# Relative-position scores with eight queries in three 128-row stationaries instead of two queries in one of 96 rows

## The chip, the cores and the metric

The kernel runs on one core of a Trainium2 chip. Times are device microseconds (us) of one execution. Five engines work side by side: TensorE (PE, with its weight loads as PEld), VectorE (DVE), ScalarE (ACT), GpSimd (POOL) and SyncE (SP), which here issues every DMA.

## The reference

An attention layer with relative positions, then a routed feed-forward layer, on 16 sequences of 1024 rows and 256 columns, 16 heads of 16. The part that the change is about are the attention scores:

```
idx = r[None, :] - r[:, None] + (MAX_LEN - 1)          # jax clips it to the table's 1023 rows
rel = rel_emb[idx]
qk = jnp.einsum('bhld,bhrd->bhlr', q, k) / np.sqrt(HEAD_DIM)
qk = qk + jnp.einsum('bhld,lrd->bhlr', q, rel)
att = jax.nn.softmax(qk, axis=-1)
out = jnp.einsum('bhlr,bhrd->bhld', att, v)
```

The first einsum is the content term, the second the rel term. For a query l the rel term needs, for each key r, the table's row r - l: a window of the table that moves by one with the query.

## The kernel before, in words

A tile is 128 queries of one sequence with all 16 heads; there are 128 tiles (8 per sequence). Within a tile 16 groups g = 0 to 15 follow each other: jp = g // 4 picks 256 of the 1024 keys, i = k = g % 4 picks 32 of the 128 queries. A group's scores fill two PSUM banks, c = 0 and 1, each 128 keys by 16 heads by 32 queries, and `scores(g, c, buf)` fills one of them. Below, one such call is called a pass; a tile has 32.

A product of float32 numbers is made of three fp16 products (high and low halves), so 16 dimensions take 48 rows of contraction, and 96 rows hold two such blocks. **Content term:** a pass has 8 matmuls, one for two heads: the stationary is `ks` (96 rows by 128 keys, the two heads above each other), the moving operand is `qm`, 64 columns, which is zero where block and head don't match. **Rel term:** a pass has 16 matmuls, one for two neighbouring queries. The stationary is 128 columns of `tw`, in which the second block of rows is the table shifted by one; the moving operand is `rm`, 16 heads by two queries, 32 columns, zero where block and query don't match. `tw_s` is the shifted table in DRAM, `raw` the six loads (SP, `load_raw`) of a tile's queries, repeated down the 96 rows. `mask(i)` on POOL makes `qm` and `rm` of 32 queries out of `raw` with two multiplications by 0/1 masks.

One group on PE, as `tile` writes it: pass c = 0 of g; a transpose of the last group's row maxima (`transpose_max`, L674, which waits on DVE's L962); pass c = 1 of g; work of other stages (`wide` and `mixed`: products with the values L693, transposes L700 and L705, projections L714); then `shift` (L683), which adds the negated maxima of the last group to its banks. In four groups of a tile with k = 1, and in g = 0 and 8, `wide` comes straight after pass c = 1. In the ten others PE first waits on `s_nmr`, which DVE's L971 raises; L971 itself needs `transpose_max`. DVE does for a group: L971 (negated maxima), L974, the reduction L962 of the group's two banks, then `side(g)`, small operations of the other stages (layer norms, router). ACT does the exponential (L847). POOL's order within a tile is written out in its `tile`: mask(3), splits of x1 and x, `wp` to `osum` (L580 to L590), `qkb` to `qkl` (L594, L547, L549), and so on, then x1 (L625), mask(0), rs2 (L541, L543), mask(1), mask(2). SP's order is written out too: the window of keys 3, `load_raw` once mask(3) is done, `xr`, windows 0 to 2, the stores.

Before the attention loop come the constants, the writes of `tw_s`, eight tiles of projections alone, and the first loads. The attention loop of every engine but SP has three tiles in its body (`passes`, NBUF = 3) and is jumped back 42 times.

Of the kernel before, what the change touches and what calls it, by code (L numbers as in the profile page):

```python
# [24 lines left out]
TWC = 3 * P  # L25
NU = 2 * L
# [3 lines left out]
NBUF = 3  # L30

# [7 lines left out]
def sandwich_kernel(nc, x, wqT, bq, wkT, bk, wvT, bv, woT, bo, relT, baseT, base_b,  # L39
# [9 lines left out]
    t_s = nc.dram_tensor("t_s", (2, HD, NU + 1), f16, kind="Internal").ap()  # L49
    tw_s = nc.dram_tensor("tw_s", (ROWS, NU), f16, kind="Internal").ap()  # L50

    ctx = ExitStack()
    with ctx:
# [11 lines left out]
        mask_q = sb("mask_q", [ROWS, H, IW], f16)  # L65
        mask_r = sb("mask_r", [ROWS, H, IW], f16)
# [132 lines left out]
        s_raw = sem("s_raw")  # L199
        s_mask = sem("s_mask")  # L200
# [82 lines left out]

        assert (NT - 2) % NBUF == 0

        def passes(eng, tile):
            tile(-TPB, 0, att=False, proj=True, a=False, b=False)
            with eng.Fori(1, TPB) as n:
                tile(n - TPB, n, att=False, proj=True, a=False, b=False)
            tile(0, TPB, att=True, proj=True, a=False, b=False, ph=0)  # L290
            tile(1, TPB + 1, att=True, proj=True, a=True, b=False, ph=1)
            with nc.Fori(2, NT, NBUF, engines=(eng.engine,), hint_back_edge=True) as t:
                for k in range(NBUF):
                    tile(t + k, t + (k + TPB), att=True, proj=True, a=True, b=True, ph=(2 + k) % NBUF)
            tile(NT, None, att=False, proj=False, a=True, b=True, ph=NT % NBUF)
            tile(NT + 1, None, att=False, proj=False, a=False, b=True)
# [3 lines left out]
        def _(sp):  # L300
# [31 lines left out]
            for s in range(2):  # L332
                for k, part in enumerate(SPLIT_ST):
                    r = (3 * s + k) * HD
                    sp.dma_start(tw_s[r:r + HD, :], t_s[part, :, 1 - s:1 - s + NU]).then_inc(s_tws, 16)
            sp.wait_ge(s_tws, 6 * 16)

            def load_window(it, jp):
                u = (TPB - 1) * P - it * P + 2 * P * jp
                sp.dma_start(tw[:, jp, :], tw_s[:, bass.ds(u, TWC)] if not isinstance(u, int)  # L340
                             else tw_s[:, u:u + TWC]).then_inc(s_tw[jp], 16)

            def load_raw(b, it):
                for s in range(2):
# [27 lines left out]
            def tile(b, it, att, proj, a, bb, new=False, last=False, end=False, wrap=False, first=False):  # L372
# [4 lines left out]
                if att:  # L377
                    if not first:

                        after(s_scores, t * NG)  # L380
                        load_window(it, NJP - 1)
                        if new:
                            after(s_qkst, n * 64)
                            load_keys(b, NJP - 1)
                    after(s_mask, t * NI + NI)
                    if last:
                        load_raw(b + 1, 0)
                    else:
                        load_raw(b, it + 1)
# [63 lines left out]
            sp.wait_ge(s_qkst, TPB * 64)  # L453
            load_raw(0, 0)
# [35 lines left out]
        def _(pool):  # L490
# [5 lines left out]
            g.memset(mask_q[:, :, :], 1.0)  # L496
            g.memset(mask_r[:, :, :], 1.0)
# [24 lines left out]
            q4 = mask_q[:, :, :].rearrange("p (h s) i -> p h s i", s=2)  # L522
            r4 = mask_r[:, :, :].rearrange("p h (i s) -> p h i s", s=2)
            keep(q4[:, :, 0, :], ALU.is_ge, half - 1, [[0, H // 2], [0, IW]], -1)
            keep(q4[:, :, 1, :], ALU.is_ge, -half, [[0, H // 2], [0, IW]], 1)
            keep(r4[:, :, :, 0], ALU.is_ge, half - 1, [[0, H], [0, IW // 2]], -1)
            keep(r4[:, :, :, 1], ALU.is_ge, -half, [[0, H], [0, IW // 2]], 1)
# [121 lines left out]
        def _(pe):  # L649
# [5 lines left out]
            def scores(g, c, buf):  # L655
# [140 lines left out]
            def tile(t, n, att, proj, a, b, ph=None):  # L796
                read = None
                for g in range(NG):
                    jp, k = divmod(g, NI)
                    old = a if g == 0 else att  # L800
                    if att:
                        if k == 0:
                            pe.wait_ge(s_tw[jp], t * 16 + 16)
                            pe.wait_ge(s_ks[jp], batch_of(t) * 96 + 96)
                        if jp == 0:
# [4 lines left out]
                        scores(g, 0, buffer(ph, g))  # L810
# [4 lines left out]
                    if att:  # L815
                        scores(g, 1, buffer(ph, g)).then_inc(s_scores, 1)
# [103 lines left out]
        def _(dve):  # L920
# [27 lines left out]
            v.memset(tf[:, 0:1], 0.0)  # L948
            v.tensor_copy(tf[:, 1:1 + MAX_LEN], relf[:, NREL - MAX_LEN:NREL])
            v.tensor_copy(tf[:, 1 + MAX_LEN:1 + MAX_LEN + NREL], relf[:, :])  # L950
            v.tensor_copy(tf[:, 1 + MAX_LEN + NREL:NU + 1],
# [157 lines left out]
```

## Time and profile before

| | |
|---|---|
| median of 3 runs | 6342.19 us (6337.41 to 6345.55) |
| profiled execution | 6342.86 us, its span 6341.1 us |
| PE busy | 5961.8 us (94%), 178176 matmuls |
| DVE busy | 4987.0 us (79%) |
| POOL busy | 3652.9 us (58%) |
| ACT busy | 3127.8 us (49%) |
| DMA | 296.74 MB, the main queue 16.0% of 16 engines' time |
| granted TensorE clock | mean 0.985; 0.94 from 100 to 300 us, 1.00 from 1000 to 1768 us |

A busy PE is not PE at its peak, since ends of matmuls are modelled: what a matmul costs in a stream is read from the distance of starts, or from the chain of work that ended last. An engine's busy share says how much room it has on average; whether it holds up another is read from what that one waited for, group by group.

### The profile page before, as it was taken

The page shows a single profiled execution, that of the slowest core. Times are in us where ns is not written, and L with a number is a line of the kernel's source. Part 1 is how long each engine was busy: PE and PEld are TensorE (multiplying, and loading weights), DVE is VectorE, ACT ScalarE, POOL GpSimd, SP SyncE. Part 2 cuts the span into 40 slices and gives each one's busy share as a digit, 9 for nine tenths or more (in the row PEclk, how much of TensorE's full clock was granted, in tenths as well). Part 3 has the DMA queues.
Part 4 walks back from the last instruction along what each step waited for, and adds up shares of the span by engine and source line. Part 5 has one row for each costly group of instructions (what it writes and reads, how often), then busy time and mean ns, then how long its engine had stood idle before and what let it go on. Part 6 is the DMA issues. An engine that isn't in the chain of part 4 may idle for free.

```text
span 6341.1 us, 408511 instructions
## 1 busy us (share of the span) xinstructions
PE 5961.8 (94%) x178176; PEld 5617.6 (89%) x178176; DVE 4987.0 (79%) x10289; ACT 3127.8 (49%) x5145; POOL 3652.9 (58%) x4709
## 2 busy tenths in 40 slices
PE   5999999999999999999999999999999999999997
PEld 4989899899998998898999899899999999998987
DVE  3787788878788887878887888888788788887786
ACT  1555455455555554555555555455555555554554
POOL 5555655565565555555655655555565556556555
PEclk7999999999999999999999999999999999999998
DMA  3111121111212112121121211112111121211211
GB/s 87 39 44 52 36 61 36 54 44 38 60 36 62 36 36 62 36 61 34 42 58 36 60 37 49 47 40 60 36 53 45 36 60 40 59 37 36 62 36 27
DMA packets 570090, 296.74 MB, mean 47 GB/s; under 512 B 384177, under 2 KB 534689, under 8 KB 568625
## 3 DMA queue, kind: packets, MB, share of 16 engines
q1 hardware_dynamic: 568624, 272.86, 16.0%
q8 instruction: 1450, 23.76, 1.6%
q14 instruction: 16, 0.12, 0.0%
HBM read 184.46 MB, written 88.60 MB: 43 GB/s over the span
## 4 chain that ended last, share of the span: by engine, by line
PE 83%; DVE 8%; issue 4%; DVEq 3%; POOLq 1%; ACT 1%; POOL 0%; SPq 0%; DMA 0%
PE sc L667 22%; PE pw L693 15%; PE sc L683 14%; PE sc L662 13%; PE pm L714 4%; PE pw L700 4%; PE pw L714 4%; PE pm L674 4%; DVE r L962 3%; DVEq L973 2%; DVE y2n L928 2%; DVE nm L971 1%; PE pm L727 1%; PE pm L705 1%; DVE gate L1005 1%
## 5 line engine op out<-in xcount | busy, mean ns | idle before, releaser
L962 DVE TRANSPOSE_TENSOR_REDUCE r<-sc 128x32 f16<-128x1024 f32 x2048 | 2548.8, 1245 | 52.0 <-PE sc L667 51.4
L667 PE MATMUL sc<-rm,tw 96*128 96x32 f16 x65536 | 2293.4, 177 | 71.6 <-issue 70.8
L847 ACT ACTIVATE prob<-sc 128x1024 f32<-128x1024 f32 x2048 | 2097.3, 1024 | 193.7 <-PE sc L683 141.3
L667 PEld LDWEIGHTS sc<-rm,tw 96*128 96x128 f16 x65536 | 1979.9, 97 | 79.5 <-issue 79.0
L662 PE MATMUL sc<-qm,ks 96*128 96x64 f16 x32768 | 1639.8, 193 | 28.8 <-DMA ks<-qk_s 15.5
L971 DVE TENSOR_REDUCE nm<-pm 16x32 f16<-16x256 f32 x2048 | 840.8, 411 | 753.7 <-PE pm L674 750.3
L662 PEld LDWEIGHTS sc<-qm,ks 96*128 96x128 f16 x32768 | 1302.8, 98 | 34.3 <-issue 34.2
L683 PE MATMUL sc<-nmm,pick 128*128 128x64 f16 x32768 | 1302.0, 193 | 2.5 <-DVE nmm L974 1.2
L683 PEld LDWEIGHTS sc<-nmm,pick 128*128 128x128 f16 x32768 | 1151.9, 98 | 122.4 <-issue 105.5
L693 PE MATMUL pw<-prob,vs 128*32 128x128 f32 x32768 | 1115.7, 277 | 129.8 <-DVE nm L971 124.7
L693 PEld LDWEIGHTS pw<-prob,vs 128*32 128x32 f32 x32768 | 842.6, 110 | 185.8 <-DVE nm L971 137.4
L974 DVE TENSOR_TENSOR nmm<-nm,mask_h 16x64 f16<-16x64 f16 x2048 | 607.6, 297 | 195.1 <-issue 9.8
L839 ACT ACTIVATE ot<-pw 128x512 f32<-128x512 f32 x512 | 305.8, 597 | 739.7 <-PE pw L693 739.7
L547 POOL TENSOR_TENSOR oT<-oT,one 128x256 f16<-128x256 f32 x128 | 78.6, 614 | 926.9 <-ACT oT L839 926.9
L535 POOL TENSOR_TENSOR rm<-raw,mask_r 96x512 f16<-96x512 f16 x515 | 608.3, 1181 | 0.0
L534 POOL TENSOR_TENSOR qm<-raw,mask_q 96x512 f16<-96x512 f16 x515 | 591.3, 1148 | 20.3 <-PE sc L667 10.4
L674 PE MATMUL pm<-ident,r 128*128 128x128 f16 x4096 | 561.5, 218 | 0.5 <-DVE r L962 0.5
L839 ACT ACTIVATE nmt<-pm 128x16 f32<-128x16 f32 x512 | 94.2, 184 | 771.1 <-PE pm L727 771.1
L700 PE MATMUL pw<-ident,ot 128*128 128x128 f32 x2048 | 322.9, 280 | 54.2 <-DVE nm L971 53.9
L839 ACT ACTIVATE parts<-pw 128x272 f32<-128x272 f32 x512 | 203.5, 397 | 327.2 <-PE pw L700 320.6
L580 POOL TENSOR_TENSOR wp<-parts,wst 128x1088 f32<-128x1088 f32 x128 | 281.6, 2200 | 113.3 <-ACT parts L839 113.3
L543 POOL TENSOR_TENSOR rs<-ve,mhalf 128x1 f32<-128x1 f32 x521 | 287.4, 552 | 74.0
(131 smaller groups left out, 5803.9 us busy)
## 6 DMA issues: line engine op xcount, KB each, us to landing
raw<-qk_s SPq DMA_DIRECT2D x774, 64.0 KB, 2.8
tw<-tw_s SPq DMA_DIRECT2D x512, 72.0 KB, 2.1
v_s<-vpad SPq DMA_DIRECT2D x136, 256.0 KB, 3.6
vs<-v_s SPq DMA_DIRECT2D x64, 512.0 KB, 3.7
ks<-qk_s SPq DMA_DIRECT2D x384, 64.0 KB, 2.5
xin<-x SPq DMA_DIRECT2D x138, 128.0 KB, 2.9
qk_s<-qkh SPq DMA_DIRECT2D x272, 64.0 KB, 1.7
qk_s<-qkl SPq DMA_DIRECT2D x272, 64.0 KB, 1.6
```

The lines of the kernel that those rows point to most:

```text
L534: g.tensor_tensor(qm[:, i, :, :], src, mask_q[:, :, :], ALU.mult)
L535: g.tensor_tensor(rm[:, i, :, :, :].rearrange("p i h s -> p h i s"), src.rearrange("p h (i s) -> p h i s", s=2), mask_r[:, :, :].rearrange ...
L662: last = mm(bank[:, 2 * h * IW:(2 * h + 2) * IW], ks[:, h, j:j + P], qm[:, i, 2 * h:2 * h + 2, :].rearrange("p h i -> p (h i)"), start=(h ...
L667: last = mm(out3[:, :, 2 * k:2 * k + 2], tw[:, jp, u:u + P], rm[:, i, k, :, :], start=False, stop=False, skip_group_check=True)
L674: last = mm(p_max[:, c * P:(c + 1) * P], r1[:, c * H:c * H + P], ident16[:, :], start=True, stop=True)
L683: last = mm(pairs[:, :, h, :], pick[:, h, :], nmm[:, :, :], start=False, stop=True, skip_group_check=True)
L693: last = mm(pw[32 * q:32 * q + 32, col * P:(col + 1) * P], vs[:, 2 * jp + c, h, :], prob[:, jp % 2, c, h, :], start=(c == 0), stop=(c == 1))
L839: return A(dst, src, ACT.Copy)
L847: A(prob[:, jp % 2, :, :, i * IW:(i + 1) * IW], sc[:, 2 * buf:2 * buf + 2, :].rearrange("p c (h i) -> p c h i", i=IW), ACT.Exp).then_inc(s ...
L962: v.tensor_reduce(r1[:, 0:2 * H], sc[:, 2 * buf:2 * buf + 2, :].rearrange("p c (h i) -> p (c h) i", i=IW), axis=AX.X, op=ALU.max, apply_tr ...
L971: v.tensor_reduce(part, p_max[0:H, :].rearrange("h (q i) -> h i q", i=IW), axis=AX.X, op=ALU.max, negate=True).then_inc(s_nmr, 1)
L974: v.tensor_tensor(nmm[0:H, :, :], part.rearrange("h (a i) -> h a i", a=1) .to_broadcast((H, 2, IW)), mask_h[:, :, :], ALU.mult).then_inc(s ...
```

## The change

The rel term now takes eight neighbouring queries at once. Their 24 blocks of 16 rows (eight queries, three fp16 parts) fill three stationaries of 128 rows. A query's 48 rows can straddle two stationaries, so the three matmuls cover queries 0 to 2, 2 to 5 and 5 to 7 of the eight: 48, 64 and 48 columns. A pass has 4 x 3 = 12 rel matmuls instead of 16, with 640 moving columns instead of 512. `tw`, `tw_s` and `raw` become three planes of 128 rows; `load_raw` has 24 loads of 64 KB instead of six, and `tw_s` is written by 24 DMAs instead of six. The content queries no longer pass through POOL: `load_queries` writes them by six DMAs of 32 KB into the blocks of `qm` where they belong, the rest of which is zeroed once; `qm` holds two tiles in turn. A mask on POOL is three multiplications of 192, 256 and 192 elements per partition instead of two of 512. Loop bodies on PE, ACT, DVE and POOL hold six tiles instead of three; SP's loops over tiles are unrolled.

```diff
+OCT = 8
+RP = 3
+RUNS = ((0, 3), (2, 4), (5, 3))
+RCOL = (0, 3, 7)
+RN = 10
+UNROLL = 2 * NBUF
...
-        tw = sb("tw", [ROWS, NJP, TWC], f16)
+        tw = sb("tw", [P, RP, NJP, TWC], f16)
-        raw = sb("raw", [ROWS, H, P], f16)
-        qm = sb("qm", [ROWS, NI, H, IW], f16)
-        rm = sb("rm", [ROWS, NI, IW // 2, H, 2], f16)
+        raw = sb("raw", [P, RP, H, P], f16)
+        qm = sb("qm", [ROWS, 2, H, P], f16)
+        rm = sb("rm", [P, NI, IW // OCT, RN * H], f16)
...
-            with nc.Fori(2, NT, NBUF, engines=(eng.engine,), hint_back_edge=True) as t:
-                for k in range(NBUF):
+            with nc.Fori(2, NT, UNROLL, engines=(eng.engine,), hint_back_edge=True) as t:
+                for k in range(UNROLL):
...
             def load_raw(b, it):
+                for k in range(RP * OCT):
+                    r = k % OCT * HD
+                    src = qk_s[SPLIT[k % 3], 0, b].rearrange("(h d) t -> d h t", d=HD)
+                    sp.dma_start(raw[r:r + HD, k // OCT, :, :], src[:, :, it * P:it * P + P]
+                                 if isinstance(it, int) else src[:, :, bass.ds(it * P, P)]).then_inc(s_raw, 16)
+
+            def load_queries(b, it):
                 for s in range(2):
                     for k, part in enumerate(SPLIT):
                         r = (3 * s + k) * HD
-                        src = qk_s[part, 0, b].rearrange("(h d) t -> d h t", d=HD)
-                        sp.dma_start(raw[r:r + HD, :, :], src[:, :, it * P:it * P + P] if isinstance(it, int)
-                                     else src[:, :, bass.ds(it * P, P)]).then_inc(s_raw, 16)
+                        src = qk_s[part, 0, b].rearrange("(h s d) t -> s d h t", s=2, d=HD)
+                        dst = qm[r:r + HD, it % 2, :, :].rearrange("p (h s) t -> p s h t", s=2)
+                        sp.dma_start(dst[:, s, :, :], src[s, :, :, it * P:it * P + P]).then_inc(s_qm, 16)
...
             def mask(i):
 
-                src = raw[:, :, i * IW:(i + 1) * IW]
-                g.tensor_tensor(qm[:, i, :, :], src, mask_q[:, :, :], ALU.mult)
-                g.tensor_tensor(rm[:, i, :, :, :].rearrange("p i h s -> p h i s"),
-                                src.rearrange("p h (i s) -> p h i s", s=2),
-                                mask_r[:, :, :].rearrange("p h (i s) -> p h i s", s=2),
-                                ALU.mult).then_inc(s_mask, 1)
+                for s, ((q, n), c) in enumerate(zip(RUNS, RCOL)):
+                    src = raw[:, s, :, i * IW:(i + 1) * IW].rearrange("p h (m e) -> p m h e", e=OCT)
+                    last = g.tensor_tensor(rm[:, i, :, c * H:(c + n) * H].rearrange("p m (h e) -> p m h e", e=n),
+                                           src[:, :, :, q:q + n],
+                                           mask_r[:, c:c + n].rearrange("p (a b e) -> p a b e", a=1, b=1)
+                                           .to_broadcast((P, IW // OCT, H, n)), ALU.mult)
+                last.then_inc(s_mask, 1)
...
-                for k in range(IW // 2):
-                    u = P - 1 - (i * IW + 2 * k) + c * P
-                    last = mm(out3[:, :, 2 * k:2 * k + 2], tw[:, jp, u:u + P], rm[:, i, k, :, :],
-                              start=False, stop=False, skip_group_check=True)
+                for m in range(IW // OCT):
+                    u = P - 1 - (i * IW + OCT * m) + c * P
+                    for s, ((q, n), r) in enumerate(zip(RUNS, RCOL)):
+                        last = mm(out3[:, :, OCT * m + q:OCT * m + q + n], tw[:, s, jp, u:u + P],
+                                  rm[:, i, m, r * H:(r + n) * H].rearrange("p (h e) -> p h e", e=n),
+                                  start=False, stop=False, skip_group_check=True)
```

On PE, one pass of the first tile, before (`sc` is the bank, `ks` and `tw` the stationaries, `qm` and `rm` the moving operands):

```order
70 L662 MATMUL sc<-qm,ks 128x64 x8
71 L667 MATMUL sc<-rm,tw 128x16x2 x16
```

and the same pass in the changed kernel:

```order
55 L681 MATMUL sc<-qm,ks 128x64 x8
56 L687 MATMUL sc<-rm,tw 128x16x3
57 L687 MATMUL sc<-rm,tw 128x16x4
58 L687 MATMUL sc<-rm,tw 128x16x3 x2
59 L687 MATMUL sc<-rm,tw 128x16x4
60 L687 MATMUL sc<-rm,tw 128x16x3 x2
61 L687 MATMUL sc<-rm,tw 128x16x4
62 L687 MATMUL sc<-rm,tw 128x16x3 x2
63 L687 MATMUL sc<-rm,tw 128x16x4
64 L687 MATMUL sc<-rm,tw 128x16x3
```

The 8 content matmuls stay; 16 rel matmuls of 32 columns have become 8 of 48 and 4 of 64.

On POOL, the end of the second tile, before, from x1 (L625 stands ahead of the first row) to the last mask, where `ve` and `rs` are rs2:

```order
93 L534 TENSOR_TENSOR qm<-raw,mask_q 96x512 [waits s_scores,s_raw]
94 L535 TENSOR_TENSOR rm<-raw,mask_r 96x16x16x2
95 L541 TENSOR_TENSOR ve<-mv,eps 128x1 [waits s_mv2]
96 L543 TENSOR_TENSOR rs<-ve,mhalf 128x1
97 L534 TENSOR_TENSOR qm<-raw,mask_q 96x512 [waits s_scores]
98 L535 TENSOR_TENSOR rm<-raw,mask_r 96x16x16x2
```

and in the changed kernel:

```order
100 L553 TENSOR_TENSOR rm<-raw,mask_r 128x4x48 [waits s_scores,s_raw]
101 L553 TENSOR_TENSOR rm<-raw,mask_r 128x4x64
102 L553 TENSOR_TENSOR rm<-raw,mask_r 128x4x48
103 L560 TENSOR_TENSOR ve<-mv,eps 128x1 [waits s_mv2]
104 L562 TENSOR_TENSOR rs<-ve,mhalf 128x1
105 L553 TENSOR_TENSOR rm<-raw,mask_r 128x4x48 [waits s_scores]
106 L553 TENSOR_TENSOR rm<-raw,mask_r 128x4x64
107 L553 TENSOR_TENSOR rm<-raw,mask_r 128x4x48
```

Two long operations of each mask have become three shorter ones, in the same places.

On SP, one tile of the changed kernel (`tw` is a window, `raw` and `qm` the queries, `xr` and `xin` rows of x):

```order
112 L348 DMA tw<-tw_s 128x3x384 [waits s_scores]
113 L364 DMA qm<-qk_s 16x8x128 [waits s_mask]
114 L364 DMA qm<-qk_s 16x8x128 x5
115 L355 DMA raw<-qk_s 16x16x128 x24
116 L410 DMA xr<-x 128x256 [waits s_x1]
117 L348 DMA tw<-tw_s 128x3x384 [waits s_scores]
118 L425 DMA xin<-x 128x256 [waits s_xn]
119 L348 DMA tw<-tw_s 128x3x384 [waits s_scores]
```

Before, the place of rows 113 to 115 was held by six loads of `raw`, and a window was 96x384.

## Rows read from the trace of the kernel before

**Rows 1.** The page: busy time, share of the span, instructions; then the chain's shares

```profile
PE 5961.8 (94%) x178176; PEld 5617.6 (89%) x178176; DVE 4987.0 (79%) x10289; ACT 3127.8 (49%) x5145; POOL 3652.9 (58%) x4709
...
PE 83%; DVE 8%; issue 4%; DVEq 3%; POOLq 1%; ACT 1%; POOL 0%; SPq 0%; DMA 0%
```

**Rows 2.** The chain in order of time: start, us, what

```profile
1396.41 0.23 PE sc L662 x8
1396.65 0.39 PE sc L667 x16
```

**Rows 3.** Timeline, g = 12: start, us, engine, line, out<-in, count [idle before]

```profile
1403.03 0.27 PE L674 MATMUL pm<-ident,r 128*128 128x128 f16 x2
...
1403.34 0.41 DVE L971 TENSOR_REDUCE nm<-pm 16x32 f16<-16x256 f32 x1 [1.11 <-PE pm L674]
...
1403.38 0.56 PE L667 MATMUL sc<-rm,tw 96*128 96x32 f16 x16
...
1403.81 0.50 PE L714 MATMUL pm<-w_base,x1T 128*128 128x256 f16 x3
```

**Rows 4.** Timeline, POOL's wp in g = 4, then all engines in g = 6

```profile
1425.39 2.24 POOL L580 TENSOR_TENSOR wp<-parts,wst 128x1088 f32<-128x1088 f32 x1 [0.32 <-ACT parts L839]
...
1432.41 1.17 POOL L549 TENSOR_TENSOR qkl<-qkb,qkh 128x512 f16<-128x512 f32 x1
1432.48 1.15 DVE L1011 TENSOR_TENSOR cgt<-gate 128x36 f32<-128x36 f32 x1
1433.55 0.41 DVE L971 TENSOR_REDUCE nm<-pm 16x32 f16<-16x256 f32 x1
...
1434.01 0.54 PE L693 MATMUL pw<-prob,vs 128*32 128x128 f32 x12 [1.05 <-DVE nm L971]
```

**Rows 5.** Timeline, g = 15 and on into the next tile: y2n beside mask(0)

```profile
1410.45 1.15 POOL L534 TENSOR_TENSOR qm<-raw,mask_q 96x512 f16<-96x512 f16 x1
...
1411.56 1.16 POOL L535 TENSOR_TENSOR rm<-raw,mask_r 96x512 f16<-96x512 f16 x1
1411.56 1.30 DVE L928 TENSOR_SCALAR y2n<-y,mv,rs 128x256 f32<-128x256 f32 x1
...
1412.79 0.41 DVE L971 TENSOR_REDUCE nm<-pm 16x32 f16<-16x256 f32 x1
...
1413.25 0.44 PE L700 MATMUL pw<-ident,ot 128*128 128x128 f32 x2 [0.49 <-DVE nm L971]
...
1414.57 0.37 DVE L928 TENSOR_SCALAR xn<-x,mv,rs 128x256 f32<-128x256 f32 x1
...
1415.85 0.38 PE L705 MATMUL pm<-ident,xn 128*128 128x128 f32 x2
```

**Rows 6.** Groups of instructions by shape: busy us, mean ns | idle before

```profile
L535 POOL TENSOR_TENSOR rm<-raw,mask_r 96x512 f16<-96x512 f16 x515 | 608.3, 1181 | 0.0
L534 POOL TENSOR_TENSOR qm<-raw,mask_q 96x512 f16<-96x512 f16 x515 | 591.3, 1148 | 20.3 <-PE sc L667 10.4 <-DMA raw<-qk_s 9.9
...
L928 DVE TENSOR_SCALAR y2n<-y,mv,rs 128x256 f32<-128x256 f32 x128 | 112.3, 877 | 1.0 <-POOL rs L543 1.0
...
L625 POOL TENSOR_TENSOR x<-yn,xr 128x256 f32<-128x256 f32 x128 | 94.8, 740 | 1.2 <-DVE yn L928 1.2
```

**Rows 7.** The line L580, all 128 of them: duration, first and last start

```profile
L580 POOL TENSOR_TENSOR wp<-parts,wst x128: 2037/2229/2238, 169.9 to 6303.8; 128x1088 f32<-128x1088 f32 x128
```

**Rows 8.** SP's timeline: start of the run, then three places of tiles

```profile
29.18 3.77 SPq L335 DMA_DIRECT2D tw_s<-t_s  x6
...
403.21 0.34 SPq L444 DMA_DIRECT2D out<-res  x1
...
450.46 0.34 SPq L444 DMA_DIRECT2D out<-res  x1
...
1421.40 3.02 SPq L348 DMA_DIRECT2D raw<-qk_s  x6
```

**Rows 9.** Waits: engine, line, waited for: us in total, times, longest

```profile
PE sc L662 <- DMA ks<-qk_s: 15.5, 1, 15.5
```

**Rows 10.** The page: DMA queue, packets, MB, share of 16 engines

```profile
q1 hardware_dynamic: 568624, 272.86, 16.0%
```

More of the change, by code:

```diff
@@ L48, in sandwich_kernel @@
     v_s = nc.dram_tensor("v_s", ((B + 1) * TPB, P, H * 32), f32, kind="Internal").ap()
-    t_s = nc.dram_tensor("t_s", (2, HD, NU + 1), f16, kind="Internal").ap()
-    tw_s = nc.dram_tensor("tw_s", (ROWS, NU), f16, kind="Internal").ap()
+    t_s = nc.dram_tensor("t_s", (2, HD, NU + OCT - 1), f16, kind="Internal").ap()
+    tw_s = nc.dram_tensor("tw_s", (RP, P, NU), f16, kind="Internal").ap()
     ctx = ExitStack()
@@ L199, in sandwich_kernel @@
         s_raw = sem("s_raw")
+        s_qm = sem("s_qm")
         s_mask = sem("s_mask")
@@ L291, in passes @@
             tile(1, TPB + 1, att=True, proj=True, a=True, b=False, ph=1)
-            with nc.Fori(2, NT, NBUF, engines=(eng.engine,), hint_back_edge=True) as t:
-                for k in range(NBUF):
-                    tile(t + k, t + (k + TPB), att=True, proj=True, a=True, b=True, ph=(2 + k) % NBUF)
-            tile(NT, None, att=False, proj=False, a=True, b=True, ph=NT % NBUF)
+            with nc.Fori(2, NT, UNROLL, engines=(eng.engine,), hint_back_edge=True) as t:
+                for k in range(UNROLL):
+                    tile(t + k, t + (k + TPB), att=True, proj=True, a=True, b=True, ph=2 + k)
+            tile(NT, None, att=False, proj=False, a=True, b=True, ph=NT % UNROLL)
             tile(NT + 1, None, att=False, proj=False, a=False, b=True)
@@ L331, in _ @@
             sp.wait_ge(s_tst, 32)
[L332 to L336, printed above, removed]
+            for k in range(RP * OCT):
+                q, part = divmod(k, 3)
+                r = k % OCT * HD
+                sp.dma_start(tw_s[k // OCT, r:r + HD, :],
+                             t_s[SPLIT_ST[part], :, OCT - 1 - q:OCT - 1 - q + NU]).then_inc(s_tws, 16)
+            sp.wait_ge(s_tws, RP * OCT * 16)
             def load_window(it, jp):
                 u = (TPB - 1) * P - it * P + 2 * P * jp
-                sp.dma_start(tw[:, jp, :], tw_s[:, bass.ds(u, TWC)] if not isinstance(u, int)
-                             else tw_s[:, u:u + TWC]).then_inc(s_tw[jp], 16)
+                src = tw_s.rearrange("s p u -> p s u")
+                sp.dma_start(tw[:, :, jp, :], src[:, :, bass.ds(u, TWC)] if not isinstance(u, int)
+                             else src[:, :, u:u + TWC]).then_inc(s_tw[jp], 16)
             def load_raw(b, it):
+                for k in range(RP * OCT):
+                    r = k % OCT * HD
+                    src = qk_s[SPLIT[k % 3], 0, b].rearrange("(h d) t -> d h t", d=HD)
+                    sp.dma_start(raw[r:r + HD, k // OCT, :, :], src[:, :, it * P:it * P + P]
+                                 if isinstance(it, int) else src[:, :, bass.ds(it * P, P)]).then_inc(s_raw, 16)
+            def load_queries(b, it):
                 for s in range(2):
@@ L386, in tile @@
                     if last:
+                        load_queries(b + 1, 0)
                         load_raw(b + 1, 0)
                     else:
+                        load_queries(b, it + 1)
                         load_raw(b, it + 1)
@@ L453, in _ @@
             sp.wait_ge(s_qkst, TPB * 64)
+            sp.wait_ge(s_cpool, 1)
+            load_queries(0, 0)
             load_raw(0, 0)
@@ L462, in _ @@
             tile(0, 1, True, True, True, False)
-            with sp.Fori(2, TPB - 1) as it:
+            for it in range(2, TPB - 1):
                 tile(0, it, True, True, True, True)
@@ L469, in batch @@
                 tile(b, 0, True, True, True, True, new=True, wrap=wrap)
-                with sp.Fori(1, TPB - 1 - turn) as it:
+                for it in range(1, TPB - 1 - turn):
                     tile(b, it, True, True, True, True, wrap=wrap)
@@ L521, in _ @@
             half = ROWS // 2
[L522 to L527, printed above, removed]
+            for (q, n), c in zip(RUNS, RCOL):
+                lo = q * half - c // 3 * P
+                keep(mask_r[:, c:c + n], ALU.is_ge, -lo, [[-half, n]], 1)
+                pool.drain()
+                keep(mask_r[:, c:c + n], ALU.is_ge, lo + half - 1, [[half, n]], -1)
             keep(tri[:, :, :], ALU.is_gt, 0, [[1, E], [-1, E]], 0)
@@ L804, in tile @@
                             pe.wait_ge(s_ks[jp], batch_of(t) * 96 + 96)
+                        if g == 0:
+                            pe.wait_ge(s_qm, t * 96 + 96)
                         if jp == 0:
@@ L945, in _ @@
             normal(xn[:, :], xin[:, :], mv0, rs0).then_inc(s_xn, 1)
[L948 to L951, printed above, removed]
+            v.memset(tf[:, 0:OCT - 1], 0.0)
+            v.tensor_copy(tf[:, OCT - 1:OCT - 1 + MAX_LEN], relf[:, NREL - MAX_LEN:NREL])
+            v.tensor_copy(tf[:, OCT - 1 + MAX_LEN:OCT - 1 + MAX_LEN + NREL], relf[:, :])
+            v.tensor_copy(tf[:, OCT - 1 + MAX_LEN + NREL:NU + OCT - 1],
                           relf[:, NREL - 1:NREL].to_broadcast((HD, NU - MAX_LEN - NREL)))
```

27 lines of the change are left out of this document (13 added, 14 removed).

## The prediction

> **What bounds the kernel now.** I read the page first, then the chain of work that ended last, then the timeline of one ordinary tile group by group. The page has PE busy 94% of the span, and the chain that ended last lies on PE for 83% of it, on DVE and its queue for 11% [rows 1]. So PE's stream is the bound, with places where PE waits for DVE, and both kinds of place have to be counted. The chain in order of time prices a pass: the 8 content matmuls take 0.23 us, 29 ns each for 64 columns, and the 16 rel matmuls 0.39 us, 24.4 ns each for 32 columns [rows 2]. Half the columns cost nearly the same, so below about 64 columns a matmul with its weight load has a price of its own, and fewer of them should be cheaper.
>
> An ordinary tile lasts 47.25 us (from one store of `out` to the next, 403.21 to 450.46 [rows 8]).
>
> **Rel matmuls.** Removed: 16 x 24.4 = 390 ns a pass. Added: four of 64 columns at 29 ns and eight of 48 columns. For 48 columns no row exists; they lie between the 24.4 ns of 32 columns and the 29 ns of 64 [rows 2]. I take the lower end, since the 29 ns of 64 columns look like a price per column (64 columns in 29 ns are 0.45 ns each, so 48 would be 22 ns, under the floor). New: 4 x 29 + 8 x 24.4 = 312 ns. Gain 78 ns a pass; with the upper end 12 x 29 = 349 ns and a gain of 41 ns. There are 4096 passes, so 320 us if all of it counted.
>
> The Trainium skill, "TensorE: Matmul & The Clock Gate", section LDWEIGHTS, prices a weight load at P / 1.2 ns with P its columns, 107 ns for 128, however many rows. By it a rel block would be 1.7 us, and four loads less a pass would be worth 4096 x 0.43 = 1750 us. The trace contradicts it: load and matmul together come every 24.4 ns here [rows 2], and the sum goes by that.
>
> **How much of it counts.** A pass that PE finishes sooner counts only if PE doesn't then wait. Take g = 12 [rows 3]: `transpose_max` starts at 1403.03, DVE's L971 is done at 1403.34 + 0.41 = 1403.75, and PE's next matmul starts at 1403.81. Pass c = 1 ends at the same moment: its last rel matmul starts about 0.39 us after 1403.38. So after `transpose_max` PE has just enough work to cover L971, and a shorter pass c = 1 only makes PE wait on `s_nmr`. That holds for the ten groups in which that wait comes straight after pass c = 1: ten of the 32 passes are lost. The six others (k = 1, and g = 0 and 8) have `wide` first.
>
> Groups 4 to 6 hang on another chain. POOL starts wp at 1425.39 once ACT has its parts, and runs wp, osum, qkb, qkh, qkl with hardly a gap to 1432.41 + 1.17 = 1433.58. DVE's cgt, 36 elements per partition, starts with qkl and takes 1.15 us: it ends with it. L971 follows, and PE, which has waited 1.05 us, goes on at 1434.01 [rows 4]. From PE's transposes of g = 3 to this point everything is fixed by POOL, so pass c = 0 of g = 4, 5, 6 and c = 1 of g = 5 are lost too: four. Group 15 has a stall of the same kind, priced next; its pass c = 0 is left out here. That leaves 32 - 10 - 4 - 1 = 17 passes, 17 x 0.078 = 1.33 us. I take off 0.13 us for the groups 8 and 9, in which DVE has its longest side work after group 6 and may become last, and for pv waiting on the exponential: **1.2 us a tile**.
>
> **Masks.** POOL's price per element: 256 float32 elements take 740 ns, 512 fp16 elements 1148 or 1181 ns, the strided one hardly more [rows 6]; so about 0.3 us + 1.7 ns per element. 192, 256 and 192 elements make 0.6 + 0.74 + 0.6 = 1.95 us a mask instead of 2.33. Ends: 1.1 us (0.37 each) if the price is per element only at the best row, 3.5 us if each costs as much as the long ones do now. The masks themselves wait for nothing that is late (idle before them 20.3 us in the whole run [rows 6]) and PE never waits for them. What they do is to hold up DVE. At the end of a tile y2n starts at 1411.56 beside the second half of mask(0) and takes 1.30 us, ending just behind it; L971 comes after, and PE has waited 0.49 us when it starts L700 at 1413.25 [rows 5]. Its mean over all tiles is 877 ns [rows 6], the xn of the same size takes 0.37 us. With three operations of 0.6 to 0.74 us the same y2n meets an operation that ends about 1411.7 instead of 1412.7. If it gets in then, the stall is gone, with 0.08 us of pass c = 0: 0.57 us; if it falls behind the third, about 0.2 us. I take **0.45 us a tile**.
>
> **Loop bodies.** 128 starts of wp lie between 169.9 and 6303.8 us [rows 7]: 6133.9 us for 127 tiles, of which 47.25 x 127 = 6000.8 is ordinary. The remaining 133 us I put down to the 42 jumps back, 3.2 us each. With 21 jumps left, the gain is **67 us**; the ends are 0 (a body twice as long costs twice as much to get going) and 67.
>
> **Loads.** Six DMAs take SP 3.02 us, 0.5 us each [rows 8]. A tile now has 30 in that place, 15 us, so xr, windows and xin behind them go out 12 us later. `raw` is issued at about 1421 and must have landed at mask(0), which before starts 37 us later in the tile (1410.45 + 47.25 = 1457.7 [rows 5, 8]); the windows behind it are for the next tile. So in the loop it is hidden, and becomes last only if a DMA takes over 1.2 us to issue. A packet costs 6341 x 16 x 0.16 / 568624 = 28.5 ns of an engine [rows 10]; 18 loads of 256 packets more, 6 of 128, and 1152 more for the windows are 6528 a tile, 11.6 us on 16 engines out of 47. At the start nothing hides them: the 18 more writes of `tw_s` at 3.77 / 6 = 0.63 us hold up SP by 11 us [rows 8], ahead of the next rows of x, and PE already waits 15.5 us for the first keys [rows 9], which now stand behind 24 more loads, 12 to 13 us. Together **+24 us**; the lower end is 12, if SP catches up with the projections.
>
> **The sum.** The profiled execution took 6342.86 us (span 6341.1), 0.7 above the median. (1.2 + 0.45) x 126 ordinary tiles = 208; 6343 - 208 - 67 + 24 = 6092, rounded to **6090 us**.
>
> **The rivals.**
> *Forecast, chance 0.6:* as above, 6040 to 6150.
> *All passes count, 0.08:* DVE comes earlier as a whole and no wait takes the gain. (32 x 0.078 + 0.57) x 126 = 387, so 6343 - 387 - 67 + 24 = 5913 us. Against it speaks that L971 ends with the pass at g = 12 [rows 3].
> *Half the gain, 0.2:* 48 columns cost what 64 do (17 x 0.041 - 0.1 = 0.6 us a tile: 6343 - 132 - 67 + 24 = 6168), or the jumps back cost as much in all as before (6157). With both, 6235.
> *POOL becomes last, 0.08, the slower side:* the mask now reads runs of three or four elements, which no row shows. From x1 the order is mask(0), rs2, then xn, then PE's transposes: xn is done at 1414.94 and PE uses it at 1415.85 [rows 5], so mask(0) may grow by 0.9 us for nothing, to 3.2. At 3.5 us the tile loses 0.3 and the 0.45 of the stall, 6090 + 95 = 6185. The kernel gets slower once mask(0) takes over 3.2 + 1.5 = 4.7 us, which eats the 1.2 us and the jumps; at 2.2 us an operation it is 6.6 us, and 3.4 x 126 = 428 more against gains of 194: 6577 us.
> *Loads are late, 0.04:* instruction fetches and 30 DMAs share the queues' engines in the first 15 us of each tile, where the jump back falls too. If each tile loses 2 us to that, 6090 + 252 = 6342, no change. Against it: 16% of the engines' time is in use [rows 10].
>
> The Trainium skill, "DMA: Bandwidth & Descriptors", section Bandwidth, speaks for this last one: it calls transfers under 64 KB dominated by descriptors and gives 0.95 us to one of 64 KB. As an estimate from that page 24 loads would need 23 us of all engines; that is still under the 37 us. Here six such loads are issued in 3.02 us [rows 8].
>
> **Chances and range.** No change that a measurement can tell is within 0.2%, 13 us. Faster: the first three and most of the rest that is not slower, 0.87; same 0.03; slower 0.10, from the last two. The range leaves out the far end of the second rival and the slower ones: 5985 to 6235.
>
> **What would show it.** Right: rel blocks of 0.31 us on the chain; 0.09 us waits of PE for L971 in about ten groups of a tile; y2n near 0.5 us and no wait at L700; POOL's three operations near 0.6, 0.74 and 0.6 us; ordinary tiles of 45.6 us; 21 long ones; PE's first wait near 28 us. Wrong: rel matmuls at 29 ns or more, masks over 3 us, a tile whose POOL chain from wp to qkl is met by PE earlier and moves, or new waits marked issue outside the jumps.

## The result: 1.8% faster, under half of the gain that was forecast

The changed kernel takes 6225.19 us (median of 4, 6219.34 to 6235.45) against 6341.91 us for the kernel before on the same chip: a ratio of 0.982 (0.980 to 0.984), so 117 us faster. The forecast was 6090 us, a gain of 252. The profiled execution took 6235.45 us, 107 less than the profiled one of before, and the account below is made between those two.

The page of the changed kernel, with busy time, then the chain's shares and lines, then the main DMA queue (packets, MB, share of 16 engines):

```profile
PE 5857.5 (94%) x161792; PEld 5428.1 (87%) x161792; DVE 4998.5 (80%) x10289; ACT 3139.6 (50%) x5145; POOL 3362.3 (54%) x5226
...
PE 73%; DVE 13%; issue 6%; DVEq 6%; POOLq 1%; ACT 1%; POOL 0%; SPq 0%; DMA 0%
```

```profile
q1 hardware_dynamic: 1459696, 565.02, 36.0%
```

PE is still 94% busy with 16384 matmuls fewer, but its share of the chain fell from 83% to 73% and that of DVE with its queue rose from 11% to 19% [rows 1]: PE now arrives first more often. The DMA queue is more than twice as busy [rows 10].

The chain in order of time, ordinary groups (start, us, what), the answer to [rows 2]:

```profile
1576.43 0.24 PE sc L681 x8
1576.66 0.36 PE sc L687 x12
1577.02 0.74 PE pm L735 x6
```

Twelve rel matmuls take 0.36 us, where sixteen took 0.39. The distances of starts in the trace are 29 to 30 ns for every one of them, 48 columns and 64 alike. The forecast block was 0.31 us.

The tile's end, start, us, engine, line, out<-in, the answer to [rows 5]:

```profile
1586.41 1.72 POOL L553 TENSOR_TENSOR rm<-raw,mask_r 128x192 f16<-128x192 f16 x3
...
1587.50 0.78 DVE L951 TENSOR_SCALAR y2n<-y,mv,rs 128x256 f32<-128x256 f32 x1
...
1588.99 3.45 POOL L553 TENSOR_TENSOR rm<-raw,mask_r 128x192 f16<-128x192 f16 x6
...
1589.98 0.88 DVE L951 TENSOR_SCALAR xn<-x,mv,rs 128x256 f32<-128x256 f32 x1
...
1591.28 0.56 DVE L997 TENSOR_TENSOR nmm<-nm,mask_h 16x64 f16<-16x64 f16 x1
...
1591.89 0.64 PE L704 MATMUL sc<-nmm,pick 128*128 128x64 f16 x16 [0.21 <-DVE nmm L997]
```

y2n did not get in between two operations of mask(0): it ends 0.15 us behind the last of them (1586.41 + 1.72 = 1588.13), as it did before (1412.86 behind 1412.72 [rows 5]). So it does in 102 of 128 tiles here and in 126 before, where it took 1.3 us in 41 tiles and 0.7 in 85: its length only says how early it started. What freed PE is that the whole mask takes 1.72 us instead of 2.27: PE's wait for nm ahead of the transposes of `ot` (L700 before, L721 now) fell from 53.9 us in the run to 4.6. But the two DVE operations that fall beside the next POOL run, mask(1) and mask(2) in six operations without a gap, take 0.88 us (xn, 0.37 before [rows 5]) and 0.56 us (nmm, 0.18 where POOL is quiet). Both hold up what follows; PE's wait for nmm at L704 is 22.4 us in the whole run, where it was 1.2.

Groups by shape (busy us, mean ns | idle before), the answer to [rows 6]:

```profile
L553 POOL TENSOR_TENSOR rm<-raw,mask_r 128x192 f16<-128x192 f16 x1030 | 612.8, 600 | 33.9 <-DMA raw<-qk_s 22.4 <-PE sc L687 11.5
L553 POOL TENSOR_TENSOR rm<-raw,mask_r 128x256 f16<-128x256 f16 x515 | 314.0, 610 | 0.0
...
L951 DVE TENSOR_SCALAR xn<-x,mv,rs 128x256 f32<-128x256 f32 x128 | 110.4, 863 | 3.2 <-POOL rs L562 3.2
L951 DVE TENSOR_SCALAR y2n<-y,mv,rs 128x256 f32<-128x256 f32 x128 | 89.0, 695 | 1.0 <-POOL rs L562 1.0
```

The starts of wp (duration; first and last start), the answer to [rows 7], and the wait for the first keys, the answer to [rows 9]:

```profile
L599 POOL TENSOR_TENSOR wp<-parts,wst x128: 2036/2146/2193, 187.0 to 6191.5; 128x1088 f32<-128x1088 f32 x128
```

```profile
PE pw L714 <- DVE nm L994: 132.8, 126, 1.1
...
PE sc L681 <- DMA ks<-qk_s: 27.2, 1, 27.2
```

**Where the 107 us come from.** First to last wp takes 6004.5 us instead of 6133.9. The median tile without a jump back fell from 47.27 to 46.68 us, 127 x 0.59 = 75 us. What the tiles with a jump back take over that median fell from 127.5 us in 42 to 64.5 us in 21, 63 us. The other tiles' excess grew from 2.8 to 11.0 us, 8 us lost. The first wp comes 17.1 us later, and what lies behind the last wp grew by some 5 us. 75 + 63 - 8 - 22 = 108 us. The same terms in the forecast were 208, 67, 0 and 24: of the 144 us that are missing, 133 are missing inside the ordinary tile.

### The profile page after: what moved, and what is told of

Its sections match the earlier page's. It is cut to its first block, busy times and chain, and to the rows that moved or that the text cites. A ratio compares the mean times of both kernels' runs of the same rounds, so it can differ in the third digit from the quotient of the medians.

```text
span 6233.7 us, 379790 instructions
## 1 busy us (share of the span) xinstructions
PE 5857.5 (94%) x161792; PEld 5428.1 (87%) x161792; DVE 4998.5 (80%) x10289; ACT 3139.6 (50%) x5145; POOL 3362.3 (54%) x5226
## 4 chain that ended last, share of the span: by engine, by line
PE 73%; DVE 13%; issue 6%; DVEq 6%; POOLq 1%; ACT 1%; POOL 0%; SPq 0%; DMA 0%
PE sc L687 18%; PE pw L714 14%; PE sc L704 13%; PE sc L681 12%; DVE r L985 5%; PE pm L735 5%; DVEq L996 4%; PE pw L735 4%; PE pm L695 3%; PE pw L721 3%; DVE xn L951 2%; DVE nm L994 1%; DVE nmm L997 1%; DVE y2n L951 1%; PE pm L748 1%
## 5 line engine op out<-in xcount | busy, mean ns | idle before, releaser
L687 PE MATMUL sc<-rm,tw 128*128 128x48 f16 (+1 forms) x49152 | 2152.1, 195 | 37.3 <-issue 37.0
L687 PEld LDWEIGHTS sc<-rm,tw 128*128 128x128 f16 x49152 | 1758.7, 100 | 42.5 <-issue 41.8
L681 PE MATMUL sc<-qm,ks 96*128 96x64 f16 x32768 | 1637.9, 193 | 37.7 <-DMA ks<-qk_s 27.2
L704 PE MATMUL sc<-nmm,pick 128*128 128x64 f16 x32768 | 1299.1, 193 | 28.9 <-DVE nmm L997 22.4
L704 PEld LDWEIGHTS sc<-nmm,pick 128*128 128x128 f16 x32768 | 1146.1, 98 | 167.9 <-issue 104.5
L714 PE MATMUL pw<-prob,vs 128*32 128x128 f32 x32768 | 1111.2, 276 | 143.4 <-DVE nm L994 132.8
L714 PEld LDWEIGHTS pw<-prob,vs 128*32 128x32 f32 x32768 | 838.8, 110 | 221.0 <-DVE nm L994 148.0
L553 POOL TENSOR_TENSOR rm<-raw,mask_r 128x192 f16<-128x192 f16 (+1 forms) x1545 | 886.7, 603 | 33.9 <-DMA raw<-qk_s 22.4
L997 DVE TENSOR_TENSOR nmm<-nm,mask_h 16x64 f16<-16x64 f16 x2048 | 583.9, 285 | 204.7 <-issue 19.4
L599 POOL TENSOR_TENSOR wp<-parts,wst 128x1088 f32<-128x1088 f32 x128 | 274.4, 2144 | 173.3 <-ACT parts L862 173.3
L560 POOL TENSOR_TENSOR ve<-mv,eps 128x1 f32<-128x1 f32 x521 | 113.8, 218 | 420.4 <-DVE mv L948 420.0
L721 PE MATMUL pw<-ident,ot 128*128 128x128 f32 x2048 | 323.4, 281 | 11.0 <-DVE nm L994 4.6
```

Of the source, the lines that this page charges most:

```text
L553: last = g.tensor_tensor(rm[:, i, :, c * H:(c + n) * H].rearrange("p m (h e) -> p m h e", e=n), src[:, :, :, q:q + n], mask_r[:, c:c + n]. ...
L687: last = mm(out3[:, :, OCT * m + q:OCT * m + q + n], tw[:, s, jp, u:u + P], rm[:, i, m, r * H:(r + n) * H].rearrange("p (h e) -> p h e", e=n),
L704: last = mm(pairs[:, :, h, :], pick[:, h, :], nmm[:, :, :], start=False, stop=True, skip_group_check=True)
L714: last = mm(pw[32 * q:32 * q + 32, col * P:(col + 1) * P], vs[:, 2 * jp + c, h, :], prob[:, jp % 2, c, h, :], start=(c == 0), stop=(c == 1))
L997: v.tensor_tensor(nmm[0:H, :, :], part.rearrange("h (a i) -> h a i", a=1) .to_broadcast((H, 2, IW)), mask_h[:, :, :], ALU.mult).then_inc(s ...
```

## Experiments

Ratios are against the kernel before on the same chip. That kernel's time differs a little from chip to chip: its median was 6338.03, 6334.44 and 6324.61 us in the three sets of runs, so differences across sets are taken from the ratios. Where a kernel ran only once, its time stands alone. The first four are about the price of a rel matmul.

**48 columns cut to 32** (one of the three queries in each run of three gets no rel term; two columns per head are written):

```diff
+    w = 2 if n == 3 else n
-    last = mm(out3[:, :, OCT*m+q:OCT*m+q+n], ..., rm[..., r*H:(r+n)*H]...
+    last = mm(out3[:, :, OCT*m+q:OCT*m+q+w], ..., rm[..., r*H:(r+w)*H]...
```

> The changed kernel, but the eight matmuls of 48 columns in a pass take only 32 of them (two of three queries are computed, the third is left out). In the changed kernel all twelve rel matmuls of a pass start 29 to 30 ns apart, 0.36 us a block. Theory 'columns' (48 columns cost what 64 do, 32 columns cost less): eight of the twelve fall to 24 or 25 ns, block 0.31 to 0.32 us. Theory 'rows' (the 128-row stationary sets the price): stays at 0.36 us. Theory 'overlap' (neighbouring matmuls that add into the same columns of a bank hold each other up): some gain too, since a third of the overlap is gone, but no clean 24 ns. Rounds are not needed: the block's time on the chain decides.

Measured: 6210.79 us; the block is 0.34 us, the distances of starts 26 to 29 ns. A fifth of the moving columns is worth 0.02 us, which is less than the theory of columns expected (0.31 to 0.32) and more than the theory of rows did. The matmuls of 32 columns cost 29 ns ahead of one of 64 and 26 ns ahead of one of 32, where a row of sixteen such matmuls, with the same 16 short runs of two columns, has 24.4 ns each [rows 2].

**96 rows contracted instead of 128** (a quarter of each rel product is left out): `tw[:ROWS, ...]` and `rm[:ROWS, ...]` in the rel matmul.

> The changed kernel, but rel matmuls contract only the first 96 of the 128 rows (a quarter of the products is left out). Theory 'rows': the block falls from 0.36 to about 0.30 us. Theories 'columns', 'runs' and 'overlap': stays at 0.36 us and the kernel's time within 10 us of the changed one's.

Measured: 6241.46 us, block 0.36 us. The rows have no part in it.

**Each rel matmul writes one unbroken stretch of the bank** (same sizes, sums in the wrong columns):

```diff
-    last = mm(out3[:, :, OCT*m+q:OCT*m+q+n], ..., rm[..., r*H:(r+n)*H].rearrange("p (h e) -> p h e", e=n),
+    last = mm(bank[:, (OCT*m+q)*H:(OCT*m+q+n)*H], ..., rm[..., r*H:(r+n)*H],
```

> The changed kernel, but each rel matmul writes its 48 or 64 columns as one run instead of 16 runs of 3 or 4 (sums land in wrong columns of the bank; nothing is left out). Theory 'runs' (writing short runs costs): block falls below 0.33 us. The others: stays at 0.36 us.

Measured: 6188.60 us. The chain of this kernel, start, us, what:

```profile
1613.53 0.47 PE sc L704 x16
1614.23 0.32 PE sc L687 x12
1614.90 0.32 PE sc L687 x12
```

The block is 0.32 us, 25 to 26 ns for 48 columns and 28 ns for 64. So the shape of the write is what costs here: 16 short runs of three elements, one per head, cost as much as 16 runs of four, 29 to 30 ns; the same 48 columns in one run are near the floor that the forecast took. The number of runs alone isn't the price, since 16 runs of two elements have 24.4 ns in the kernel before [rows 2]. Why three cost what four do, and two don't, no run here shows.

**The three planes in the outer loop**, so that matmuls in a row don't read neighbouring stationaries (same result):

> The changed kernel with the twelve rel matmuls of a pass in another order: all four of stationary plane 0, then of plane 1, then of plane 2, so that no two neighbours add into the same columns. Same result. Theory 'overlap': block falls below 0.33 us and the kernel gains up to 50 us. The others: stays at 0.36 us, time within 10 us of the changed kernel's.

Measured: 6242.22 us, block 0.36 us: the order has no part in it.

**Loop bodies alone.** The kernel before with six tiles in a body (`UNROLL = 2 * NBUF`), nothing else:

> The kernel before with nothing changed but the loop bodies: six tiles instead of three. Theory 'jumps' (a jump back costs some 3 us whatever stands in the body): 21 jumps fewer, 6342 - 64 = 6278 us, 6268 to 6288. Rival (the price grows with the body, or comes from the loads that fall beside it): 6330 to 6342.

Measured: 6281.37 us, ratio 0.991 (0.990 to 0.993), 53 us. The term for the jumps is confirmed by itself.

**Masks in the middle of the tile.** `rm` gets two buffers, and the four masks move off the tile's end to places between POOL's operations of the middle:

```diff
-        rm = sb("rm", [P, NI, IW // OCT, RN * H], f16)
+        rm = sb("rm", [P, 2, NI, IW // OCT, RN * H], f16)
...
+                if att:
+                    mask(1, (ph + 1) % 2)
+                    mask(2, (ph + 1) % 2)
```

> The changed kernel with two buffers of rm, so that a tile's four masks run in the middle of the tile before (one after vpad, two after hT's split, one after y) instead of around the tile's end. Theory 'moved stall' (the shorter masks freed y2n at g = 15, but xn and L997 then wait for the six masks that now stand back to back, and PE loses at g = 0 what it gained at g = 15): the 0.47 us at g = 0 goes too, ordinary tile 46.1 us, about 60 us less than the changed kernel, 6165 us. Rival (DVE's side work at g = 9 to 12 is hit instead): 6215 to 6250.

Measured: 6741.39 us, ratio 1.064 (1.062 to 1.065), ordinary tile 50.96 us. Both expectations missed, and widely. The rival had the place right (the periods of nm in g = 11 and 12 grow by 3.5 and 1.3 us) and not the size. Here xn and y2n are back at 0.38 us in the mean, but another operation of DVE is hit. The timeline:

```profile
1639.73 3.40 POOL L553 TENSOR_TENSOR rm<-raw,mask_r 128x192 f16<-128x192 f16 x6
...
1641.24 4.28 DVE L998 TENSOR_TENSOR nmm<-nm,mask_h 16x64 f16<-16x64 f16 x1
...
1643.08 0.73 POOL L636 TENSOR_TENSOR y<-y,b_o 128x256 f32<-128x256 f32 x1
1643.76 1.72 POOL L553 TENSOR_TENSOR rm<-raw,mask_r 128x192 f16<-128x192 f16 x3
1645.45 1.23 DVE L986 TRANSPOSE_TENSOR_REDUCE r<-sc 128x32 f16<-128x1024 f32 x1
1645.58 0.58 PE L705 MATMUL sc<-nmm,pick 128*128 128x64 f16 x14 [3.11 <-DVE nmm L998]
```

nmm, a product of 64 elements per partition that takes 0.18 us when POOL is quiet, takes 4.28 us: it begins beside the third of ten POOL operations in a row and ends at 1645.52, with the last of them (1645.48). The Trainium skill, "SBUF — State Buffer", section SBUF: two separate sides, has a VectorE operation with two SBUF inputs and a GpSimd one exclude each other, the first holding the shared ports for its whole instruction. The direction agrees. But by that rule nmm would wait for the rest of one instruction of about 0.6 us; here it waits through seven more.

**cgt one group later.** In [rows 4] DVE's cgt (two SBUF inputs, 36 elements) meets qkl. It moves from behind g = 5 to g = 6, where POOL pauses:

```diff
                    v.tensor_tensor(ceq[:, :, :], gf, ge, ALU.is_equal)
-                    v.tensor_tensor(cgt[:, :, :], gf, ge, ALU.is_gt)
                 if g == 6 and b:
+                    v.tensor_tensor(cgt[:, :, :], gf, ge, ALU.is_gt)
```

> The changed kernel with DVE's cgt moved from g = 5 to g = 6, behind that group's L994, L997 and reduction, so that L994 of g = 6 doesn't wait for cgt, which waits for POOL's qkl. Same result. If the waits of g = 4 to 6 are as the prediction read them (everything fixed from wp to qkl), about 1.0 us a tile of PE's 1.28 us wait goes: 6225 - 127 = about 6100 us. Rival (DVE is the bound from g = 6 to 10, or gate alone still waits for POOL): 6170 to 6225.

Measured: 6129.63 us, ratio 0.968 (0.967 to 0.969), tile 45.87 us. The group of cgt has a mean of 152 ns instead of 1115, and the 132.8 us that PE waited at L714 for DVE's nm are gone. Placing one 36-element operation is worth 1.4%, beside the 1.8% of the whole change.

**Both moves together:**

> e6 and e7 together. If the two stalls are apart in the tile the gains add: about 6225 - 60 - 127 = 6040 us. If DVE becomes the bound between them the sum is less: 6080 to 6150.

Measured: 6666.69 us, ratio 1.053 (1.051 to 1.055). Both expectations missed again: against the masks' move alone 75 us of cgt's gain stay, and the loss of the masks stays too.

**A pause of POOL between mask operations**, in three kernels: on the changed kernel, on the one with cgt moved, and on the one with both moves.

```diff
                for s, ((q, n), c) in enumerate(zip(RUNS, RCOL)):
+                    if s:
+                        pool.drain()
...
                last.then_inc(s_mask, 1)
+                pool.drain()
```

> e8 (masks in the middle of the tile before, cgt in g = 6) with drains between the mask operations. Theory 'unbroken run': the 3 to 5 us waits of L997 fall below 0.6 us each and with them some 3.5 us a tile: 6667 - 450 = about 6200 us or less, down to 6060 if DVE's work in g = 9 to 12 has room. Rival (it is the place, not the unbroken run): above 6400.

Measured: 6099.91 us, ratio 0.964 (0.962 to 0.965), where the same kernel without the drains has 1.053: some 560 us. No work was taken off either engine, so it is the lack of gaps in POOL's run that held up DVE. Without the drains PE waited 388.3 us for nmm, 128 times; with them it waits 1.2 us, four times.

From the kernel with cgt moved to this one, the three periods of DVE's nm around the tile's end go from 3.04, 2.58 and 2.60 us to 2.88, 2.33 and 2.24 (medians): 0.77 us a tile was the price of the masks' place, and the ordinary tile is 45.42 us. It is the best version of this study, 3.6% under the kernel before.

> The changed kernel with a drain on POOL between the three multiplications of a mask and behind the last. Same result. In e6 one L997 of DVE waited 4.28 us behind nine mask operations and y that followed each other without a gap, and ended with the last; where POOL drains (as in front of qkh) its trace has idle gaps of 0.2 us. Theory 'unbroken run' (a DVE operation with two SBUF inputs, or xn, gets in only where POOL's queue leaves a gap): with gaps after each 0.6 us operation xn and L997 wait at most one operation, the stall of g = 0 shrinks by 0.3 to 0.5 us a tile, 40 to 60 us less than the changed kernel: 6165 to 6185 us. Rival (each single operation holds DVE up whatever lies between): unchanged, 6215 to 6240.

Measured: 6309.70 us, ratio 0.997 (0.996 to 0.998), some 1.5% worse than the changed kernel (0.982), where a gain was expected. At the tile's end, with the masks where they are in the changed kernel, all went as expected:

```profile
L954 DVE TENSOR_SCALAR xn<-x,mv,rs 128x256 f32<-128x256 f32 x128 | 53.3, 417 | 0.8 <-POOL rs L565 0.8
L954 DVE TENSOR_SCALAR y2n<-y,mv,rs 128x256 f32<-128x256 f32 x128 | 51.7, 404 | 1.0 <-POOL rs L565 1.0
```

The three periods of nm there fall from 3.04, 2.58 and 2.59 us to 2.88, 2.33 and 2.28, and PE's wait for nmm from 22.4 us in the run to 1.4. The stall came back elsewhere. The drains make a mask 2.1 us instead of 1.72, POOL ends the tile later, and goes straight from rs into wp:

```profile
1614.32 0.55 POOL L565 TENSOR_TENSOR rs<-ve,mhalf 128x1 f32<-128x1 f32 x1
...
1614.84 2.04 POOL L602 TENSOR_TENSOR wp<-parts,wst 128x1088 f32<-128x1088 f32 x1
...
1614.91 2.12 DVE L954 TENSOR_SCALAR xn<-xin,mv,rs 128x256 f32<-128x256 f32 x1 [0.48 <-POOL rs L565]
1616.95 0.41 DVE L997 TENSOR_REDUCE nm<-pm 16x32 f16<-16x256 f32 x1
...
1617.41 1.46 PE L738 MATMUL pw<-xT,w_q 128*128 128x128 f16 x12 [2.00 <-DVE nm L997]
```

```profile
PE pw L738 <- DVE nm L997: 186.6, 100, 2.0
```

The other xn had its place between rs and wp, because wp waited for ACT's parts (173.3 us of idle time before wp in the changed kernel, 38.5 here). Now it starts 0.07 us behind wp's start and lasts as long as wp, 1655 ns in the mean instead of 448. Behind it on DVE stands nm, and PE waits 100 times, up to 2.00 us, and behind a quarter of these waits the clock fell too (see below). In periods of nm, one group grows by 1.5 us in the mean and the next by 0.3; g = 6 and the tile's end give back 1.2.

> e7 with the drains of e9. Gains at different places of the tile add: 6130 - 50 = 6080 us. If the drains do nothing: 6120 to 6135.

Measured: 6286.85 us, ratio 0.994 (0.993 to 0.996). The expectation missed: the gains don't add, and against the kernel with cgt moved alone (0.968) the drains lose 2.6%, by the same xn (mean 1672 ns). Of cgt's gain hardly anything is left, since in the kernel with drains alone the period that cgt had lengthened has fallen from 4.19 to 3.41 us already (medians); here it is 3.30.

**Six of the 24 loads of `raw`** in each tile behind the first (three quarters of the later rel terms use old queries):

> The changed kernel with six of the 24 loads of raw per tile after the first tile (three quarters of the rel queries stay those of the first tile: left out). Same instructions on PE, DVE, POOL and ACT. If the loads cost nothing in the loop, as the prediction has it: 6215 to 6235 us. If they lengthen the jumps back and the small stalls on instruction supply: 20 to 60 us less, 6165 to 6205.

Measured: 6212.32 us, ratio 0.982 (0.981 to 0.984), where the changed kernel has 0.982. So the 18 loads more per tile have no cost that these runs can tell: the 13 us between the two medians are less than the 17 us by which the kernel before differs between the two chips. The ordinary tile stays (46.61 us, 46.68 in the changed kernel). The excess of the tiles with a jump is 49.5 us instead of 64.5, but it lies between 56 and 66 us in the four kernels of the first set too, so one trace doesn't show that the loads moved it.

## Why the prediction was wrong in its size

**Rel matmuls: the step that failed first.** "I take the lower end" for 48 columns. The upper end was right, 29 to 30 ns, and the argument for the lower ("the 29 ns of 64 columns look like a price per column") failed because it counted columns and left out the shape of the write. With the same columns in one stretch, 64 cost 28 ns and 48 cost 25 to 26: in that shape the argument would nearly have held. The gain per pass was 0.048 us with its surroundings (a pass of 0.357 us instead of 0.405), not 0.078.

**How many passes count: right.** The rule of 17 gives 17 x 0.048 - 0.13 = 0.69 us a tile. In periods of nm (medians), the thirteen groups away from the tile's end got shorter by up to 0.09 us each, 0.66 us together, and the waits of about 0.1 us behind nm are there. 0.66 / 0.048 makes 14 of 32 passes that counted; in the kernel with unbroken writes, whose pass is 0.034 us shorter again, the same thirteen groups give 0.44 us, 13 passes. So this term is 0.69 and not 1.2: 0.5 x 126 = 64 us of the missing 144.

**Masks and the stall: the second step that failed.** The operations of 192 elements cost 600 ns in the mean, as forecast; the one of 256 cost 610 and not 740, and a mask is 1.72 us and not 1.95. The stall at the end of g = 15 went, 0.45 us off its period, as large as forecast, but not in the way that was forecast: y2n did not get in ahead of the mask's last operation. It still ended 0.15 us behind it, the case that the step priced at 0.2, and the mask was 0.55 us shorter. Here the step's number was right by luck. But the next two periods grew by 0.21 each. The step asked which POOL operation y2n meets, and took the DVE operations behind it at their old durations. Those were good only by their place. POOL's timeline of the kernel before, beside the xn of [rows 5] (1414.57 to 1414.94):

```profile
1413.57 1.14 POOL L534 TENSOR_TENSOR qm<-raw,mask_q 96x512 f16<-96x512 f16 x1
1414.67 1.28 POOL L535 TENSOR_TENSOR rm<-raw,mask_r 96x512 f16<-96x512 f16 x1
```

xn started 0.14 us ahead of the boundary between two long operations and got in there; it is POOL's next one that took longer, 1.28 us instead of 1.15. With other operations the boundaries lie elsewhere, and xn's mean went from 377 to 863 ns, so that nm and nmm behind it come later. nmm itself, the last of the tile, has 0.5 us in the mean in both kernels. Of "0.45 us a tile" 0.03 stayed: 53 us lost. That these durations come from POOL's unbroken run is shown by the drains at the same place: xn is back at 417 ns, nmm at 195, and the three periods give 0.72 us a tile.

The two steps make 117 us of the 133 by which the ordinary tiles fell short. The last 16 us, 0.13 us a tile, are open; part of it is that medians of single groups sum to 0.68 us gained, while whole tiles have 0.59.

**Jumps: right**, 67 forecast, 63 measured and 53 in the kernel before alone. **Loads: right in kind**, 24 us forecast for the start, where the first wp comes 17.1 us later (the other 5 of the 22 lie behind the last wp); PE's first wait for keys is 27.2 us, forecast near 28. In the loop no cost of theirs can be told.

**Rivals.** "Half the gain" named the mechanism, 48 columns at the price of 64, and gave 6168; with the loss of the stall's 53 us it would be 6221, where the profiled execution took 6235. The chance of 0.2 was too small for the end of a bound that rested on no row. "All passes count", "POOL becomes last" and "Loads are late" are excluded: 14 of 32 passes counted, a mask takes 1.72 us and not over 3, and with a quarter of the loads the ratio is the same.

## What to carry to other kernels

When matmuls are near their floor, look at the shape of what each writes as well as at its columns, and price a new shape by a row with runs of the same number and length: the row of 16 runs of two would have given the same wrong 24.4 ns. Where there is no such row, carry both ends. A DVE operation with two SBUF inputs, or with a large float32 one, should start where POOL pauses: after splitting or moving POOL work look again at every one of them, with the length of the whole run as the bound and not that of one instruction.

## What the runs showed of the hardware

**A run of POOL operations starves DVE.** Beside wp alone, xn takes 2.12 us; beside ten operations in a row, nmm takes 4.28 us; with a drain between them the mean of the same nmm falls from 3.9 to 0.57 us. It happens to operations with one large float32 input in SBUF (xn, y2n) and to small ones with two inputs (nmm, cgt), while the maxima read from PSUM kept their 1.25 us. Sometimes DVE gets in at the next boundary (xn above), sometimes only at the end of the run; what decides that stays open.

**Behind some waits of PE the clock falls as well.** PEclk is the granted clock's share of 2.4 GHz, here in the kernel with drains alone, around the wait of 2.00 us (window: us, busy of PE, PEld, DVE, ACT, POOL, PEclk, DMA share, GB/s):

```profile
1614.90:1617.40 2.50, 0.52 (x18) 0.39 (x14) 2.45 (x2) 0.28 (x1) 2.34 (x2) 0.99 0.52 118
1617.40:1619.90 2.50, 2.49 (x24) 2.49 (x25) 2.33 (x4) 0.00 (x0) 1.72 (x2) 0.50 0.61 137
```

For 2.5 us after it the clock is at 1.2 GHz, and 24 matmuls that take 1.35 us in the changed kernel take 2.53. In the changed kernel, behind a wait of 1.09 us at 1609.6, the clock stayed at 1.00. A wait of 2 us doesn't always do it: of the some 100 such waits in the kernel with drains 24 have a stretch at 0.50 behind them. Of the waits of about 3.1 us for nmm in the kernel with masks in the middle most do, 109 of 118. What decides it for a single wait stays open. The stretches behind these 24 waits sum to 82 us, so at most 41 us of that kernel's loss is the clock (an estimate: half of the time at half the clock).

A jump back can have it too. Here PE stands still for 2.48 us, without a releaser, the longest such wait, and then runs at half the clock:

```profile
1641.52 0.40 PE L687 MATMUL sc<-rm,tw 128*128 128x48 f16 x4 [2.48 <-issue]
```

```profile
1643.00:1644.00 1.00, 1.00 (x23) 1.00 (x21) 0.21 (x1) 0.72 (x3) 0.61 (x1) 0.50 0.12 25
```

The clock fell in 8 of the 21 tiles with a jump, and in 20 of 42 in the kernel before. Of the 3.1 us that such a tile takes over the median, 2.0 us in the mean are waits of PE without a releaser; that the rest is the clock is likely and not shown. The mean granted clock of 0.96 in the kernels with masks in the middle, 0.986 in the changed one, is part of their loss too.
